# The order of matmuls inside a step of 64-wide linear attention: whole-array ones first, then scores, then values

## The chip, the cores and the metric

One core of one Trainium2 chip runs the whole program. The metric is the device time of one execution, in microseconds (us), as the median of several runs. TensorE is called PE here, its weight loads PEld, VectorE DVE, ScalarE ACT, GpSimd POOL.

## The reference

Two transformer blocks, written as one function of x (4, 512, 256): softmax attention, a mixture of experts, linear attention with 128-wide heads, the mixture of experts again, then **linear attention with 32 heads of width 64**, a choice-by-expert layer, latent attention and the choice-by-expert layer again. Each adds to x. Only the 64-wide linear attention is touched:

```
qkv = silu(h @ qkv_w.T);  q, k, v = split(qkv)          # per head
for each chunk:
    aw    = (q @ k.T) * diagonal_decay                   # scores
    intra = aw @ v                                       # values
    inter = (q * query_decay) @ state                    # the state's share
    state = state * block_decay + (k * key_decay).T @ v  # growing the state
    o     = intra + inter
out = (sigmoid(h @ gate_w.T) * rmsnorm(o)) @ out_w.T
```

## The kernel before, in words

The function `lin64_layer` works in 32 **units** w: eight groups of four heads (QUADS), for each of four batches. A unit has four **steps** n = 0 to 3, one per chunk of 128 positions. Each engine runs its own list of instructions in program order; rings of PSUM banks with a "full" and a "free" semaphore tie them together. Two rings matter: S (the scores, one pair of banks) and U ("out", a single bank). D (one bank) carries the turned k, the state's growth, the next batch turned and the mean square.

In a step (w, n), PE's part is written out by hand at the end of the tensor block:

- `product` (L1401): the projections of the next unit w + 1, q at n = 0, k at n = 1, v at n = 2, the gate and the transposes of k at n = 3. q, k and gate are two times six matmuls over 512 columns (L1433), v is 24 over 256 (L1426), in float32r; the transposes are L1408. `project` (L1484, matmuls L1492) takes the output projection of unit w - 1 at n = 1.
- `scores` (L1438, matmuls L1446) of the **next** step: four matmuls whose operands stand on 64 partitions, 64x128 weights, so that heads use the upper or the lower half of the array.
- `grow_state` (L1450, matmuls L1459), not at n = 3: two matmuls over the whole array.
- `output` (L1463): for each pair r of heads two value matmuls with 128x64 weights (L1477), each into one half of the partitions, and, except at n = 0, one whole-array matmul that adds the state's share (L1480):

```
for h in range(2):
    mm = nc.tensor.matmul(bank[halves[h], to], vs[...], am[...], start=True, stop=True)
if n:
    mm = nc.tensor.matmul(bank[:, to], state[...], qd[...], start=False, stop=True, ...)
```

A plain fp32 matmul is two records in the trace (so the two state matmuls of `grow_state` are four loads); a float32r one is one record.

What the other engines do in a step: ACT activates the products out of PSUM, then squares the out bank (L1582). DVE decays the turned k (`decay_k`, L1612), decays the next step's scores (`decay_scores`, L1619), updates the state (`keep_state`, L1633 and L1638), at n = 1 adds the output projection of unit w - 1 (`add_output`, L1660), in units 0, 1 and 31 does steps of a layer norm for a next batch, and then gates the out bank (`gate`, L1648), which sets U free. In units 29 to 31, at n = 3, PE computes a mean square (`mean_square`, L1513) and DVE an inverse root (`finish`) ahead of the scores and a scaling (`scale`, L1676) ahead of the gate. POOL decays q for the next step (`decay_q`, L1740) and adds squares (L1749). After n = 3 of units 0, 1 and 31 PE transposes a next batch (`turn_batch`, L1503), which waits for DVE's normalised x (L209).

Of the kernel before, what the change touches and what calls it, by code (L numbers as in the profile page):

```python
# [31 lines left out]
NT = T // P  # L32
# [942 lines left out]
CH = P  # L975
# [331 lines left out]
H5, D5 = 32, 64  # L1307
# [6 lines left out]
def lin64_layer(nc, c, loads):  # L1314
# [21 lines left out]
    vs = sb("vs", [P, 2, NT, 4 * D5])  # L1336
    ysum = sb("ysum", [P, B, NT, DM])
    squares = sb("squares", [P, B, 2, NT, CH])
    am = sb("am", [P, 2, 2, 2, CH])
# [3 lines left out]
    qd = sb("qd", [P, 2, 2, CH])  # L1343
    state = sb("state", [P, 2, 2, P])
# [5 lines left out]
    A, D, O, S, U = c.A, c.D, c.O, c.S, c.U  # L1350
# [23 lines left out]
    halves = (slice(0, D5), slice(D5, P))  # L1374
# [3 lines left out]
    def products_in(w, n):  # L1378

        if w + 1 == N:  # L1380
            return []
        names = [("q",), ("k",), ("v",), ("gate", "turn")][n]
        return [(name, w + 1, r) for r in range(2) for name in names]
# [4 lines left out]
    def next_batch(w, n):  # L1388

        if w < B - 2:  # L1390
            return w + 2, {0: (0, 1), 1: (2, 3), 2: (4, 5), 3: (6,)}[n]
        if w == N - 1:
            return 0, {0: (0, 1, 2), 1: (3, 4), 2: (5, 6), 3: ()}[n]
        return None

    with nc.Block() as block:
        @block.tensor
        def _(pe):
# [39 lines left out]
            def scores(w, n):  # L1438
                if n == 0:
                    pe.wait_ge(A.free.s, A.released(0, "k", w, 1))  # L1440
                pe.wait_ge(S.free.s, S.may_fill(0))
                pair = S.fill("scores", w, n)
                now = slice(n * CH, (n + 1) * CH)
                for r in range(2):
                    for h, rows_ in enumerate(halves):
                        mm = nc.tensor.matmul(pair[:, h, r * CH:(r + 1) * CH], kt[rows_, w % 2, r, now],  # L1446
                                              qs[rows_, w % 2, r, now], start=True, stop=True)
                mm.then_inc(S.full.s, 1)

            def grow_state(w, n):  # L1450
                if n == NT - 1:
                    return
                if n == 0:
                    pe.wait_ge(D.free.s, D.released(0, "turn", w, 1))
                    pe.wait_ge(A.free.s, A.released(0, "v", w, 1))
                pe.wait_ge(D.free.s, D.may_fill(0))
                bank = D.fill("state", w, n)
                for r in range(2):
                    mm = nc.tensor.matmul(bank[:, r * P:(r + 1) * P], kd_[:, r, n, :],  # L1459
                                          vs[:, w % 2, n, r * P:(r + 1) * P], start=True, stop=True)  # L1460
                mm.then_inc(D.full.s, 1)

            def output(w, n):  # L1463
                pe.wait_ge(S.free.s, S.released(0, "scores", w, n))
                pe.wait_ge(U.free.s, U.may_fill(0))
                bank = U.fill("out", w, n)
                if n:
                    pe.wait_ge(D.free.s, D.released(0, "state", w, n - 1))
                    m = w * (NT - 1) + n - 1
                    pe.wait_ge(c.qd_ready.s, c.qd_ready.at(0, m + 1))  # L1470
                else:
                    pe.wait_ge(c.set_up.s, c.set_up.at(0, 3))
                for r in range(2):
                    to = slice(r * CH, (r + 1) * CH)
                    for h in range(2):
                        head = 2 * r + h
                        mm = nc.tensor.matmul(bank[halves[h], to], vs[:, w % 2, n, head * D5:(head + 1) * D5],  # L1477
                                              am[:, n % 2, h, r, :], start=True, stop=True)
                    if n:
                        mm = nc.tensor.matmul(bank[:, to], state[:, (n - 1) % 2, r, :], qd[:, m % 2, r, :],  # L1480
                                              start=False, stop=True, skip_group_check=True)
                mm.then_inc(U.full.s, 1)

            def project(w):  # L1484
                u, b = units[w]
                for half in range(2):
                    pe.wait_ge(U.free.s, U.released(0, "out", w, 2 * half + 1))
                    pe.wait_ge(O.free.s, O.may_fill(0))
                    bank = O.fill("y", w, half)
                    for i in range(2 * half, 2 * half + 2):  # L1490
                        for r in range(2):
                            mm = nc.tensor.matmul(bank[:, (i % 2) * DM:(i % 2 + 1) * DM],  # L1492
                                                  gt[:, w % 2, r, i * P:(i + 1) * P], wo[:, 2 * u + r, :],
                                                  start=(r == 0), stop=(r == 1))
                    mm.then_inc(O.full.s, 1)

            def turn_batch(b, turn):
                pe.wait_ge(c.xn_ready.s, c.xn_ready.at(0, turn))
                for kd in range(KD):
                    pe.wait_ge(D.free.s, D.may_fill(0))  # L1500
                    bank = D.fill("xt", b, kd)
                    for i in range(NT):
                        mm = nc.tensor.transpose(bank[:, i * P:(i + 1) * P], c.xn[:, i, kd * P:(kd + 1) * P],  # L1503
                                                 c.ident[:])
                    mm.then_inc(D.full.s, 1)

            def mean_square(b):
                pe.wait_ge(c.sq_ready.s, c.sq_ready.at(0, (N - 2 * B + b + 1) * NT))
                pe.wait_ge(D.free.s, D.may_fill(0))
                bank = D.fill("mean square", b)  # L1510
                for i in range(NT):
                    for r in range(2):
                        mm = nc.tensor.matmul(bank[:, i:i + 1], squares[:, b, r, i, :], one, start=(r == 0), stop=(r == 1))  # L1513
                mm.then_inc(D.full.s, 1)
# [5 lines left out]
            for k, (w, n) in enumerate(steps):  # L1520
                for what in products_in(w, n):
                    product(*what)
                if n == 1 and w:
                    project(w - 1)
                if n == 3 and w > N - B:
                    mean_square(w - 1 - (N - B))
                if k + 1 < len(steps):
                    scores(*steps[k + 1])
                grow_state(w, n)
                output(w, n)  # L1530
                if n == NT - 1 and next_batch(w, n):
                    b = next_batch(w, n)[0]
                    turn_batch(b if w < B else "next", w + 2 if w < B else B)
# [898 lines left out]
```

## Time and profile before

| what | value |
|---|---|
| median of 3 runs | 3156.69 us (3152.51 to 3158.48) |
| the profiled execution | 3153.1 us, span 3150.4 us |
| mean granted PE clock | 0.926 of full speed |
| PE busy | 2854.7 us (91%), 15592 matmuls |
| PEld busy | 1944.5 us (62%) |
| DVE busy | 1659.8 us (53%) |
| ACT busy | 842.7 us (27%) |
| POOL busy | 992.2 us (31%) |
| products of the layer, L1433 | x1152, mean 413 ns |
| scores, L1446 | x1024, mean 301 ns |
| growing the state, L1459 | x384, mean 302 ns |
| values, L1477 | x1024, mean 300 ns |
| state's share, L1480 | x384, mean 333 ns |

Busy time counts a matmul from its start to its modelled end, and matmuls overlap in the array, so a mean duration is not the distance between two of them; the starts of the weight loads show that distance. The 64-wide layer lies between about 1600 and 2475 us of the span. A load row's "idle" is the time that the load queue stood still ahead of it; "issue" names no engine or semaphore as its cause.

### The profile page before, as it was taken

The numbers are of one execution on the slowest core, as the hardware profiler recorded it, in microseconds if no ns is written. First come the engines' busy times: TensorE is split into PE (matmuls) and PEld (weight loads), VectorE is DVE, ScalarE is ACT, GpSimd is POOL, SyncE is SP. The second block draws the span as 40 slices with busy tenths as digits, with TensorE's granted clock in tenths as the row PEclk, the third lists the DMA queues.
The fourth block names the chain that finished last, engine by engine and source line by source line (L and its number), as shares of the span: only waits on it lengthen the run. The fifth ranks groups of instructions, "written<-read, shape, count | busy, mean of one in ns | idle before, by whom it ended". The sixth has DMA issues, their size and how long they took to land. (4 is left out here: it accounts for less than half of the span.)

```text
span 3150.4 us, 45793 instructions
## 1 busy us (share of the span) xinstructions
PE 2854.7 (91%) x15592; PEld 1944.5 (62%) x15592; DVE 1659.8 (53%) x4517; ACT 842.7 (27%) x1368; POOL 992.2 (31%) x1105
## 2 busy tenths in 40 slices
PE   7999999998999999999979999999999758888876
PEld 3444458886656555788867777777777634443444
DVE  5566646666555646466644333333333565555555
ACT  2343344442101101344422222222222002222310
POOL 0000036765444445567631122222221011121211
PEclk8999999999999999999989999999999657888975
DMA  3000020000000000100000000000000000000000
GB/s 138 1 0 0 0 100 1 0 0 0 1 0 0 0 0 0 81 0 0 0 14 14 1 14 15 14 1 14 15 1 1 24 0 1 1 0 1 1 0 27
DMA packets 6288, 37.96 MB, mean 12 GB/s; under 512 B 272, under 2 KB 4368, under 8 KB 4496
## 3 DMA queue, kind: packets, MB, share of 16 engines
q1 hardware_dynamic: 6160, 36.34, 3.0%
q8 instruction: 70, 1.15, 0.1%
q14 instruction: 58, 0.48, 0.0%
HBM read 34.24 MB, written 2.10 MB: 12 GB/s over the span
## 5 line engine op out<-in xcount | busy, mean ns | idle before, releaser
L590 PE MATMUL banks<-back 32*128 32x512 f32 (+3 forms) x1088 | 364.6, 598 | 31.4 <-DVE back L600 22.1
L365 PE MATMUL banks<-moe_parts 128*128 128x512 f32 x1536 | 368.4, 396 | 15.3 <-POOL moe_parts L445 8.5
L817 ACT ACTIVATE back<-banks 128x1024 f32<-128x1024 f32 (+3 forms) x256 | 217.0, 863 | 459.7 <-PE banks L711 459.5
L365 PEld LDWEIGHTS banks<-moe_parts 128*128 128x128 f32 x1536 | 287.7, 191 | 78.5 <-issue 20.8
L1433 PE MATMUL banks<-lin_parts 128*128 128x512 f32 x1152 | 307.5, 413 | 18.9 <-DVE lin_parts L1684 15.5
L1619 DVE TENSOR_TENSOR ffn_pack<-banks,back 128x512 f32<-128x512 f32 x128 | 88.5, 691 | 351.5 <-PE banks L1446 351.4
L711 PE MATMUL banks<-back 32*128 32x512 f32 (+3 forms) x1024 | 242.3, 586 | 19.8 <-DVE back L833 12.5
L1433 PEld LDWEIGHTS banks<-lin_parts 128*128 128x128 f32 x1152 | 213.6, 194 | 67.4 <-issue 21.0
L590 PEld LDWEIGHTS banks<-back 32*128 32x128 f32 x1088 | 135.2, 199 | 187.9 <-DVE back L604 77.8
L1749 POOL TENSOR_TENSOR ffn_pack<-ffn_pack 128x256 f32<-128x256 f32 x112 | 82.9, 740 | 498.9 <-ACT ffn_pack L1582 498.9
L604 DVE TENSOR_REDUCE back<-banks 128x1 f32<-128x512 f32 x272 | 176.5, 687 | 79.9 <-PE banks L590 75.4
L379 PEld LDWEIGHTS banks<-moe_parts 128*128 128x128 f32 x1536 | 191.0, 194 | 21.7 <-issue 21.1
L379 PE MATMUL banks<-moe_parts 128*128 128x256 f32 x1536 | 202.5, 289 | 0.9
L510 DVE TENSOR_TENSOR moe<-moe,banks 128x512 f32<-128x512 f32 x128 | 87.6, 688 | 198.9 <-PE banks L365 198.9
L450 POOL TENSOR_TENSOR moe_parts<-moe,moe_parts 128x512 fp32r<-128x512 f32 x128 | 165.8, 1296 | 10.2 <-ACT moe_parts L412 10.2
L462 POOL TENSOR_TENSOR moe_parts<-ffn_pack,moe_parts 128x512 fp32r<-128x512 f32 x128 | 165.2, 1290 | 0.6 <-ACT moe_parts L432 0.4
L890 POOL TENSOR_TENSOR back<-back,small_pack 128x512 f32<-128x512 f32 x32 | 33.2, 1039 | 418.6 <-DVE back L840 418.6
L1055 PE MATMUL banks<-xt,back 128*128 128x512 f32 x320 | 148.9, 602 | 4.6 <-DVE lin L1177 2.1
L1582 ACT ACTIVATE ffn_pack<-banks 128x256 f32<-128x256 f32 x128 | 49.2, 385 | 361.8 <-PE banks L1480 322.6
L422 ACT ACTIVATE moe<-banks 128x512 f32<-128x512 f32 x128 | 76.5, 597 | 243.4 <-PE banks L365 243.3
L1154 ACT ACTIVATE lin<-banks 128x512 f32<-128x512 f32 x64 | 38.2, 597 | 369.6 <-PE banks L1104 191.2
L902 POOL TENSOR_TENSOR pool_spare<-small_pack 128x1 f32<-128x1 f32 x128 | 24.7, 193 | 349.4 <-ACT back L817 349.1
(235 smaller groups left out, 5307.0 us busy)
## 6 DMA issues: line engine op xcount, KB each, us to landing
back<-p_raw SPq DMA_DIRECT2D x8, 1024.0 KB, 4.8
back<-p SPq DMA_DIRECT2D x1, 7696.0 KB, 21.5
ffn_pack<-ffn SPq DMA_DIRECT2D x1, 6144.0 KB, 26.8
back<-p SPq DMA_DIRECT2D x1, 5152.0 KB, 15.2
back<-p SPq DMA_DIRECT2D x2, 1792.0 KB, 8.2
out<-x SPq DMA_DIRECT2D x1, 2048.0 KB, 7.5
x<-x_in SPq DMA_DIRECT2D x1, 1536.0 KB, 12.7
small_pack<-small SPq DMA_DIRECT2D x1, 619.0 KB, 4.9
```

Of the source, the lines that this page charges most:

```text
L365: mm = nc.tensor.matmul(bank[:], up[:, n % 2, a, which, kd, :], xp[:, b, kd, :], start=((a, b, kd) == (0, 0, 0)), stop=((a, b, kd) == (1, ...
L379: mm = nc.tensor.matmul(bank[:, (i % 2) * DM:(i % 2 + 1) * DM], hp[:, (e % 2) * FC + f, a, i * P:(i + 1) * P], dn[:, e % 2, b, f, :], star ...
L450: nc.gpsimd.tensor_tensor(hp[:, n % 4, 1, :], gate[:, n % 4, :], hp[:, n % 4, 0, :], ALU.subtract)\
L462: nc.gpsimd.tensor_tensor(up[:, n % 2, 1], w_up[:, (n + 2) % UNITS], up[:, n % 2, 0], ALU.subtract).then_inc(c.up_lo.s, 1)
L510: nc.vector.tensor_tensor(gate[:, (e % 2) * FC + f, :], gate[:, (e % 2) * FC + f, :], bank[:], ALU.mult).then_inc(D.free.s, 1)
L590: nc.tensor.matmul(bank[:, 0:n], qs[head_rows[j], hg, qi * P:(qi + 1) * P], ks[head_rows[j], hg, 0:n], start=True, stop=True).then_inc(D.f ...
L604: ins = nc.vector.tensor_reduce(mx[:, qi, j:j + 1], bank[:], AX, ALU.max)
L711: mm = nc.tensor.matmul(bank[:, q0:T], ks[head_rows[j], hg, kt * P:(kt + 1) * P], qs[head_rows[j], hg, q0:T], start=True, stop=True)
L817: nc.scalar.activation(pt[:, (kt % 2) * 2 + pair, :, q0:T], two[:, :, q0:T], ACT.Exp, scale=0.25).then_inc(A.free.s, 2)
L1055: mm = nc.tensor.matmul(bank[:], w[:, kd, :], c.xt[:, kd, :], start=(kd == 0), stop=(kd == KD - 1))
L1433: mm = nc.tensor.matmul(bank[:], wp[:, a, m, kd, r * P:(r + 1) * P], xp[:, b, x, kd, :], start=((a, x, kd) == (0, 0, 0)), stop=((a, x, kd) ...
L1619: nc.vector.tensor_tensor(am[:, n % 2].rearrange("p h r i -> p h (r i)"), pair[:, :, 0:2 * CH], decay[:, units[w][0]].rearrange("p h r i - ...
```

## The change

In a step, PE now issues `grow_state` of this step, then the state's share of this step's output (`from_state`), then the scores of the next step, then the values of this step (`from_chunk`). The state's share begins the sum in PSUM: its first matmul sets `start`, and the value matmuls add to it (at n = 0, where there is no state, the values set `start`). The waits go with the instructions: those for the out bank, the state and the decayed q stand ahead of the state's share, the one for the decayed scores ahead of the values.

```diff
-            def output(w, n):
-                pe.wait_ge(S.free.s, S.released(0, "scores", w, n))
+            def from_state(w, n):
                 pe.wait_ge(U.free.s, U.may_fill(0))
                 bank = U.fill("out", w, n)
-                if n:
-                    pe.wait_ge(D.free.s, D.released(0, "state", w, n - 1))
-                    m = w * (NT - 1) + n - 1
-                    pe.wait_ge(c.qd_ready.s, c.qd_ready.at(0, m + 1))
-                else:
+                if n == 0:
+                    return
+                pe.wait_ge(D.free.s, D.released(0, "state", w, n - 1))
+                m = w * (NT - 1) + n - 1
+                pe.wait_ge(c.qd_ready.s, c.qd_ready.at(0, m + 1))
+                for r in range(2):
+                    nc.tensor.matmul(bank[:, r * CH:(r + 1) * CH], state[:, (n - 1) % 2, r, :], qd[:, m % 2, r, :],
+                                     start=(r == 0), stop=True, skip_group_check=True)
+
+            def from_chunk(w, n):
+                pe.wait_ge(S.free.s, S.released(0, "scores", w, n))
+                if n == 0:
                     pe.wait_ge(c.set_up.s, c.set_up.at(0, 3))
+                bank = U.banks[U.index["out", w, n] % len(U.banks)]
                 for r in range(2):
-                    to = slice(r * CH, (r + 1) * CH)
                     for h in range(2):
                         head = 2 * r + h
-                        mm = nc.tensor.matmul(bank[halves[h], to], vs[:, w % 2, n, head * D5:(head + 1) * D5],
-                                              am[:, n % 2, h, r, :], start=True, stop=True)
-                    if n:
-                        mm = nc.tensor.matmul(bank[:, to], state[:, (n - 1) % 2, r, :], qd[:, m % 2, r, :],
-                                              start=False, stop=True, skip_group_check=True)
+                        mm = nc.tensor.matmul(bank[halves[h], r * CH:(r + 1) * CH],
+                                              vs[:, w % 2, n, head * D5:(head + 1) * D5], am[:, n % 2, h, r, :],
+                                              start=(n == 0), stop=True, skip_group_check=True)
                 mm.then_inc(U.full.s, 1)
...
+                grow_state(w, n)
+                from_state(w, n)
                 if k + 1 < len(steps):
                     scores(*steps[k + 1])
-                grow_state(w, n)
-                output(w, n)
+                from_chunk(w, n)
```

PE, a step n = 1 in the middle of the layer, with its waits, from behind the output projection to v's products; before. L1446 are scores, L1459 the state's growth, L1477 values, L1480 the state's share, L1426 products; `out_free` is the out bank's semaphore.

```order
L1446 MATMUL banks<-back 128x128 [waits score_pair_free]
L1446 MATMUL banks<-back 128x128 x3
L1459 MATMUL banks<-ffn_pack,back 128x128 [waits d_free]
L1459 MATMUL banks<-ffn_pack,back 128x128
L1477 MATMUL banks<-ffn_pack 64x128 [waits d_free,qd_ready,out_free,score_pair_free]
L1477 MATMUL banks<-ffn_pack 64x128
L1480 MATMUL banks<-lin 128x128
L1477 MATMUL banks<-ffn_pack 64x128 x2
L1480 MATMUL banks<-lin 128x128
L1426 MATMUL banks<-lin_parts 128x256 [waits a_free]
```

The same step after the change, where L1472 is the state's share and L1483 the values:

```order
L1459 MATMUL banks<-ffn_pack,back 128x128 [waits d_free]
L1459 MATMUL banks<-ffn_pack,back 128x128
L1472 MATMUL banks<-lin 128x128 [waits qd_ready,d_free,out_free]
L1472 MATMUL banks<-lin 128x128
L1446 MATMUL banks<-back 128x128 [waits score_pair_free]
L1446 MATMUL banks<-back 128x128 x3
L1483 MATMUL banks<-ffn_pack 64x128 [waits score_pair_free]
L1483 MATMUL banks<-ffn_pack 64x128 x3
L1426 MATMUL banks<-lin_parts 128x256 [waits a_free]
```

The growth and the state's share moved ahead of the scores, and with them the wait for the out bank; the values are now four in a row.

PE, step n = 3 and the first products of the next step, before (L1408 transposes, L1433 products):

```order
L1408 MATMUL banks<-small_pack,back 128x128 x4
L1446 MATMUL banks<-back 128x128 x4
L1477 MATMUL banks<-ffn_pack 64x128 x2
L1480 MATMUL banks<-lin 128x128
L1477 MATMUL banks<-ffn_pack 64x128 x2
L1480 MATMUL banks<-lin 128x128
L1433 MATMUL banks<-lin_parts 128x512 x12
```

and after:

```order
L1408 MATMUL banks<-small_pack,back 128x128 x4
L1472 MATMUL banks<-lin 128x128 x2
L1446 MATMUL banks<-back 128x128 x4
L1483 MATMUL banks<-ffn_pack 64x128 x4
L1433 MATMUL banks<-lin_parts 128x512 x12
```

Here too the state's share stands ahead of the scores, and the values follow them without a break. The lists of the other engines and of the DMA queue are unchanged but for line numbers.

## Rows read from the trace of the kernel before

**Rows 1.** 1700 to 2400 us: PE, PEld, DVE, ACT, POOL busy (count), clock, DMA share, GB/s.
```profile
1700.00:2400.00 700.00, 700.00 (x4711) 553.37 (x4709) 254.85 (x604) 186.67 (x355) 166.88 (x211) 1.00 0.03 10
```

**Rows 2.** Waits of the weight loads, 1700 to 2400 us: total us, times, longest.
```profile
PEld banks L1480 <- issue: 28.1, 164, 0.2
```

**Rows 3.** Timeline: start us, us, engine, line, operation, tiles, count; step n = 0.
```profile
1900.85 2.62 PEld L1433 LDWEIGHTS banks<-lin_parts 128*128 128x128 f32 x12
...
1903.82 0.52 PEld L1446 LDWEIGHTS banks<-back 64*128 64x128 f32 x8 [0.35 <-issue]
...
1904.46 0.52 PEld L1459 LDWEIGHTS banks<-ffn_pack,back 128*128 128x128 f32 x4
...
1905.11 0.42 PEld L1477 LDWEIGHTS banks<-ffn_pack 128*64 128x64 f32 x8
...
1905.69 2.63 PEld L1433 LDWEIGHTS banks<-lin_parts 128*128 128x128 f32 x12 [0.17 <-issue]
```

**Rows 4.** Timeline, weight loads of steps n = 1 and n = 2.
```profile
1908.37 3.44 PEld L1492 LDWEIGHTS banks<-back 128*128 128x128 f32 x16
...
1912.13 0.52 PEld L1446 LDWEIGHTS banks<-back 64*128 64x128 f32 x8 [0.33 <-issue]
...
1912.78 0.52 PEld L1459 LDWEIGHTS banks<-ffn_pack,back 128*128 128x128 f32 x4
...
1913.42 0.20 PEld L1477 LDWEIGHTS banks<-ffn_pack 128*64 128x64 f32 x4
...
1913.79 0.30 PEld L1480 LDWEIGHTS banks<-lin 128*128 128x128 f32 x2 [0.17 <-issue]
...
1914.21 0.20 PEld L1477 LDWEIGHTS banks<-ffn_pack 128*64 128x64 f32 x4
...
1914.58 0.30 PEld L1480 LDWEIGHTS banks<-lin 128*128 128x128 f32 x2 [0.17 <-issue]
...
1914.80 2.94 PEld L1426 LDWEIGHTS banks<-lin_parts 128*128 128x128 f32 x24
```

**Rows 5.** Timeline, weight loads from n = 3 to the next unit.
```profile
1920.53 1.22 PEld L1433 LDWEIGHTS banks<-lin_parts 128*128 128x128 f32 x6
...
1921.79 0.59 PEld L1408 LDWEIGHTS banks<-small_pack,back 128*128 128x128 f32 x4
...
1922.35 1.24 PEld L1433 LDWEIGHTS banks<-lin_parts 128*128 128x128 f32 x6
...
1923.62 0.59 PEld L1408 LDWEIGHTS banks<-small_pack,back 128*128 128x128 f32 x4
...
1924.37 0.52 PEld L1446 LDWEIGHTS banks<-back 64*128 64x128 f32 x8 [0.17 <-issue]
...
1925.02 0.20 PEld L1477 LDWEIGHTS banks<-ffn_pack 128*64 128x64 f32 x4
...
1926.39 2.62 PEld L1433 LDWEIGHTS banks<-lin_parts 128*128 128x128 f32 x12
```

**Rows 6.** Timeline, DVE in step n = 1: decay of scores and gate.
```profile
1912.90 0.69 DVE L1619 TENSOR_TENSOR ffn_pack<-banks,back 128x512 f32<-128x512 f32 x1 [6.25 <-PE banks L1446]
...
1915.74 0.41 DVE L1648 SCALAR_TENSOR_TENSOR back<-back,banks 128x256 f32<-128x256 f32 x1
```

**Rows 7.** Timeline, the layer's two ends.
```profile
1661.37 4.53 PEld L1433 LDWEIGHTS banks<-lin_parts 128*128 128x128 f32 x12 [1.88 <-DVE lin_parts L1596]
...
2443.93 0.93 PEld L1446 LDWEIGHTS banks<-back 64*128 64x128 f32 x8
...
2449.55 0.41 DVE L1648 SCALAR_TENSOR_TENSOR back<-back,banks 128x256 f32<-128x256 f32 x1
...
2450.09 0.67 PEld L1477 LDWEIGHTS banks<-ffn_pack 128*64 128x64 f32 x8 [0.22 <-issue]
...
2460.76 0.25 PEld L1477 LDWEIGHTS banks<-ffn_pack 128*64 128x64 f32 x4 [2.14 <-issue]
```

**Rows 8.** Stretch 1661 to 1665 us, columns as in rows 1.
```profile
1661.00:1665.00 4.00, 3.63 (x9) 2.85 (x10) 0.32 (x1) 0.60 (x1) 0.00 (x0) 0.50 0.00 0
```

## The prediction

> **What bounds the kernel now.** The page's slices say that TensorE (PE) is busy nearly all the time; the question is what happens in the stage that the change touches. I read the stretches first. From 1700 to 2400 us, inside the 64-wide layer, PE is busy in 700.00 of 700.00 us at granted clock 1.00 (2.4 GHz), DVE in 254.85, ACT in 186.67, POOL in 166.88 [rows 1]. So PE sets this stage's time, and whatever PE issues less is gained, as long as nobody becomes late. A busy row counts a matmul from start to modelled end, though, and hides how far apart matmuls start. The waits list for the weight loads gives the hint: in that stretch 164 of the loads for the state's matmuls (L1480) stand behind 0.17 us in which the load queue waits for nothing named, 28.1 us together [rows 2]. That is no semaphore; it sits where a 128x128 matmul follows a 128x64 one.
>
> Then I read one unit (one group of four heads of one batch, steps n = 0 to 3) on the weight loads, whose starts show the true pitch. Call P the step's products, G the growing of the state, S the scores (64 rows), V the values (64 columns), St the state's share; G, St and P use the whole array. The unit runs from 1900.85 to 1926.39, 25.54 us [rows 3, 5].
> - St is two loads. Before another whole-array matmul it takes 1914.80 - 1914.58 = 0.22; before V it takes 1914.21 - 1913.79 = 0.42 [rows 4]. The change of shape costs 0.20.
> - G is four such loads, so 0.43 bare, and takes 0.64 before V [rows 4]: 0.21 for the change.
> - V takes 0.37 for four loads and 0.58 for eight [rows 3, 4]. Four more loads cost 0.21, so the bare eight are 0.42 and leaving V costs 0.16. The halves run in pairs.
> - S takes 0.65, before G [rows 3, 4] and before V at n = 3 [rows 5] alike.
> - P to S also costs: twelve 512-wide loads take 2.97 to S, but 2.68 to the projection, which is whole-array [rows 3, 4]. Four transposes take 0.56 to the next product and 0.75 to S [rows 5], so 0.19.
>
> Waits that are already met cost nothing here: the transposes wait for two semaphores, and the six loads ahead of them take 1.26, 0.21 each [rows 5].
>
> The Trainium skill, TensorEngine Tiling (Array Packing), Key Properties, says that changing the tiling mode, not just the tile, drains TensorE; the trace agrees with 0.16 to 0.3 us at each change. The page TensorE: Matmul & The Clock Gate, Single matmul latency, puts what a lone warm matmul pays over its columns at 166 ns. An estimate from that page alone, over the nine changes counted below and 32 units, would be 9 x 0.166 x 32 = 48 us of gain; the rows give the sum that I use.
>
> **The change, part by part.** No instruction is added or removed; the arithmetic, ACT's, DVE's, POOL's and the DMA queue's own orders stay. PE's order within a step becomes P, G, St, S, V. Changes of shape per unit, before: n = 0 four (P-S, S-G, G-V, V-P), n = 1 and 2 six each, n = 3 five, together 21. After: three per step, 12. Step by step, from the start of P's loads to the start of the next P's:
> - n = 0: before 1905.69 - 1900.85 = 4.84 [rows 3]. After: P 2.68, G 0.43, change 0.21, S 0.65, V 0.58 = 4.55. Gain 0.29.
> - n = 1: before 1914.80 - 1905.69 = 9.11 [rows 3, 4]. After: P 2.68; the projection's 16 loads at (3.44 - 0.19) / 15 = 0.217 each, 3.47 [rows 4]; G 0.43; St 0.43 + 0.20; S 0.65; V 0.58 = 8.44. Gain 0.67.
> - n = 2: before 1920.53 - 1914.80 = 5.73 [rows 4, 5]. After: 24 loads at (2.94 - 0.19) / 23 = 0.1196, 2.87 [rows 4]; then 0.43 + 0.63 + 0.65 + 0.58 = 5.16. Gain 0.57.
> - n = 3: before 1926.39 - 1920.53 = 5.86 [rows 5]. After: up to S 3.84, less 0.19; then 0.63 + 0.65 + 0.58 = 5.51. Gain 0.35.
>
> Sum 1.88 per unit. Two prices are not in the trace. P to G is a product in fp32r followed by plain fp32 of the same shape: its ends are nothing (as P to the projection) and 0.3 (as P to S); I take nothing, since the shape is what it shares with the projection. V that adds to what St began instead of overwriting: its ends are nothing and a loss of the pairing, 4 x 0.107 = 0.43 a step; I take nothing, because each fp32 matmul here is already two records, the second adding to the first, and the pairing is there.
>
> **What gets later.** St waits for the out bank (its one buffer is released by DVE's gate of the step before), and now stands ahead of S; before, that wait stood behind S and G. Behind it are queued S, and so DVE's decay of the next scores and the next state. Tightest is n = 1 to n = 2, where DVE does decay, keep_state, the output's addition and only then the gate. Before, S starts at 1912.13, DVE's decay at 1912.90 and the gate ends at 1915.74 + 0.41 = 1916.15 [rows 4, 6], 4.02 after S; add 0.13 until PE goes on (gate end 2449.96, V 2450.09 [rows 7]): 4.15. After the change PE comes to that wait S 0.65 + V 0.58 + P 2.87 + G 0.43 = 4.53 after S. Slack 0.38, so no stall. At the other steps DVE has no additions to do (over 1.2 us less) and the slack is larger. S now starts later against the end of P (0.43 + 0.63 instead of 0.2), but decayed scores are used a whole step later. ACT squares right after V as before. POOL's decayed q is made a step ahead.
>
> The ends of the layer go otherwise, since DVE is the later one there:
> - Units 0 and 1: after n = 3 PE transposes the next batch and waits for DVE's normalised x, which comes behind the decay of S. S comes 0.63 - 0.19 = 0.44 later after P, so n = 3 loses 0.44 instead of gaining 0.35: 1.09 each, 2.2 together.
> - Unit 29: the root and the scaling ahead of the gate put its end at 2449.96 when S started at 2443.93, 6.03 later, in the same chain at unit 30's end [rows 7]. After the change, from the end of the mean square: 0.63 + 0.65 + 0.58 + 2.68 + 0.43 = 4.97 against 6.03: a stall of 1.1. Unit 29 gains 0.8.
> - Units 30 and 31: unit 31 has no products as cover. S follows each late gate instead of preceding it, and the decay, the norm steps and the gate after it move too. The values of step 2 stand idle for 2.14 until that gate now [rows 7]; S, 0.65 at full clock, comes behind it twice, at half clock more. I take 1.5 of gain for unit 30 and 2 of loss for unit 31, by estimate.
>
> Sum: 27 x 1.88 = 50.8, plus 2.2, 0.8 and 1.5, less 2.0: 53.3 us. The profiled execution took 3153.1 (span 3150.4 and 2.7 around it), so 3099.8; the median of the runs is 3.6 above it: **3103 us**, 1.7% less.
>
> **The rivals.**
> 1. *The product's format costs.* P to G keeps 0.3 at n = 0 and 0.2 at n = 2. Then 0.5 a unit is lost, 14 us over 27 units: 3117. For it: PE's long waits before S follow products. Against: P to the projection shows none [rows 3, 4].
> 2. *Adding values lose the pairing.* Three steps by 0.43 over 31 units are 40 us: 3143. For it: no V in the trace adds to another matmul's sum. Against: the second pass of each does.
> 3. *Slower: the single out bank becomes the loop.* Place: the wait ahead of St at n = 2. If the gate came 1.4 us later than I count, PE would idle 1 us per unit, and idling can bring the clock down: at 1661 us, after loads that waited 1.88, the granted clock is 0.50 (1.2 GHz) [rows 8], and twelve loads took 4.53 [rows 7] instead of 2.62 [rows 3]. At 2 us of idle and 2 us of slow product a unit pays 4.0 and gains 1.88: 27 x 2.1 = 57 us slower, 3214. It decides from 2.3 us of delay without the clock's part. Against: slack 0.38, DVE busy for 36% of the stretch [rows 1]. For: all its terms come from one unit's rows, and the wait now holds S back, which feeds the same DVE queue.
> 4. *The gain is eaten.* The drain moves instead of going away (a change from 64 rows to 64 columns being dearer than the 0.22 seen at n = 3, or PE's queue bounding elsewhere): about 3157.
>
> **How the numbers follow.** My case 0.85, rival 1 0.04, rival 2 0.04, rival 3 0.04, rival 4 0.03. A unit's gain is uncertain by 0.15 (rounding of some ten differences of 0.01, and the drain's 0.16 to 0.3), 4 us; the ends by 3; the median of runs by 3. With room for half of rival 1: 3095 to 3114. A change of 0.2%, 6.3 us, is what a measurement of this kernel can tell from none. Faster: the case, rivals 1 and 2, 0.93; same: most of rival 4, 0.03; slower 0.04.
>
> **What would show it.** The unit's period in the middle falls from 25.54 to about 23.7, PE still without idle. Loads: G 0.43 to St, St 0.63 to S, S 0.65 to V, V 0.58 to P at every n; no load of St waits 0.17. P to G leaves no gap (else rival 1); V of 0.85 or more is rival 2; idle of St's loads behind DVE's gate at n = 2 in the middle of the layer is rival 3. DVE's gate ends about 4.0 after S at n = 1. I am wrong if the period is above 24.4, or if the stages outside the layer move.

## The result and the profile after

The changed kernel took 3103.96 us (median of 4 runs, 3097.37 to 3112.98) against 3156.43 us; the ratio is 0.9837, 95% interval 0.9803 to 0.9871. Faster, clear of the noise though by less than 2%: 52.5 us in the medians; 3103 was forecast, in a range of 3095 to 3114. Its runs fall into two groups, two at 3097.4 and two at 3110.5 and 3113.0. The profiled one is the longest of them: 3112.98, span 3111.2, 39.2 under the span before. A second set of runs on one chip (experiment e5) gave 3113.49 against 3153.93, ratio 0.9873 (0.9857 to 0.9889). One of its nine runs of the kernel before was slow, at 13369 us, and is not in the ratio. Of all ten runs of the change that are on record, seven lie between 3108 and 3118 and three near 3098. So the size depends on which of them are met, 40 or 52 us, and part of the closeness of the forecast is luck. Where both come from is told below.

The middle of the layer, as in [rows 1]:

```profile
1700.00:2340.00 640.00, 640.00 (x4600) 540.23 (x4600) 247.08 (x590) 182.90 (x348) 164.28 (x207) 1.00 0.03 11
```

PE is busy in 640.00 of 640.00 us at clock 1.00, as before. The busy share tells nothing of the gain: the same work now takes less time at the same 100%. The waits of the weight loads (total us, times, longest) answer to [rows 2]. Before, from 1700 to 2400 us, the loads of the scores had one more such row:

```profile
PEld banks L1446 <- issue: 23.3, 82, 0.4
```

After, from 1650 to 2400 us:

```profile
PEld banks L1433 <- issue: 15.4, 89, 0.3
PEld banks L1426 <- issue: 5.1, 30, 0.2
...
PEld banks L1472 <- DVE back L1653: 0.8, 1, 0.8
```

The 28.1 us ahead of the loads of the state's share are gone, and of the 23.3 us ahead of the scores 0.4 are left. Nearly all that remains of that kind stands ahead of products, 15.4 and 5.1 us: the change of shape from the values. The state's share (now L1472) waits for DVE's gate once in this stretch.

The timeline of a unit in the middle, weight loads, with two PE rows and DVE's gate where they are spoken of; it answers to [rows 3 to 6]. L1459 is the growth, L1472 the state's share, L1446 the scores, L1483 the values, L1426 and L1433 products:

```profile
1900.27 0.63 PEld L1459 LDWEIGHTS banks<-ffn_pack,back 128*128 128x128 f32 x4
...
1900.82 0.53 PEld L1472 LDWEIGHTS banks<-lin 128*128 128x128 f32 x4
...
1901.47 0.52 PEld L1446 LDWEIGHTS banks<-back 64*128 64x128 f32 x8
...
1902.70 2.93 PEld L1426 LDWEIGHTS banks<-lin_parts 128*128 128x128 f32 x24 [0.17 <-issue]
...
1905.04 0.42 DVE L1653 SCALAR_TENSOR_TENSOR back<-back,banks 128x256 f32<-128x256 f32 x1
1905.56 0.53 PEld L1459 LDWEIGHTS banks<-ffn_pack,back 128*128 128x128 f32 x4
...
1906.01 0.53 PEld L1472 LDWEIGHTS banks<-lin 128*128 128x128 f32 x4
...
1907.89 1.23 PEld L1433 LDWEIGHTS banks<-lin_parts 128*128 128x128 f32 x6 [0.17 <-issue]
...
1909.16 0.58 PEld L1408 LDWEIGHTS banks<-small_pack,back 128*128 128x128 f32 x4
...
1912.84 0.42 PEld L1483 LDWEIGHTS banks<-ffn_pack 128*64 128x64 f32 x8
...
1913.42 2.63 PEld L1433 LDWEIGHTS banks<-lin_parts 128*128 128x128 f32 x12 [0.17 <-issue]
...
1916.10 0.64 PEld L1459 LDWEIGHTS banks<-ffn_pack,back 128*128 128x128 f32 x4
1916.32 0.60 PE L1459 MATMUL banks<-ffn_pack,back 128*128 128x128 f32 x4
...
1916.86 0.52 PEld L1446 LDWEIGHTS banks<-back 64*128 64x128 f32 x8
...
1917.50 0.41 PEld L1483 LDWEIGHTS banks<-ffn_pack 128*64 128x64 f32 x8
...
1918.09 2.61 PEld L1433 LDWEIGHTS banks<-lin_parts 128*128 128x128 f32 x12 [0.17 <-issue]
```

From one v product to the next it is 1926.63 - 1902.70 = 23.93 us, where it was 25.55; 27 of these intervals in a row read 23.92 or 23.93. Step by step, from the start of a product to the next product's: n = 0 takes 1918.09 - 1913.42 = 4.67, n = 2 takes 1907.89 - 1902.70 = 5.19, n = 3 takes 1913.42 - 1907.89 = 5.53, and the rest, n = 1, 8.54. Against the kernel before that is 0.17, 0.54, 0.33 and 0.57 us less, for 1, 3, 2 and 3 changes of shape fewer: 0.17 to 0.19 for each, in every step. At n = 1 the gate ends at 1905.04 + 0.42 = 1905.46 and the next state's share starts at 1906.01, so the out bank is free in time.

The whole layer, from the first v load (L1426) to the first transposes of the layer behind it (L1872 before, L1877 after), reads from these rows (minimum, median and longest ns, then first and last start); first the kernel before:

```profile
L1426 PEld LDWEIGHTS banks<-lin_parts x768: 187/192/193, 1620.9 to 2434.3; 128*128 128x128 f32 x192
L1872 PE MATMUL banks<-small_pack,xn x32: 421/421/477, 2495.5 to 3076.2; 128*128 128x128 f32 x32
```

and after:

```profile
L1426 PEld LDWEIGHTS banks<-lin_parts x768: 186/192/193, 1621.7 to 2388.4; 128*128 128x128 f32 x192
L1877 PE MATMUL banks<-small_pack,xn x32: 417/421/474, 2452.5 to 3036.9; 128*128 128x128 f32 x32
```

That is 2495.5 - 1620.9 = 874.6 us before and 2452.5 - 1621.7 = 830.8 us after: 43.8 less. The two layers behind it, whose code is untouched, run from that first row's start to its last: 580.7 us before (3076.2 - 2495.5) and 584.4 after (3036.9 - 2452.5), 3.7 more; and the layer began 0.8 later. 43.8 - 3.7 - 0.8 is the 39.2 of the spans, to 0.1.

### The profile page after: what moved, and what is told of

It is laid out like the page before. It is cut to its first block and busy times, and to the rows that moved or that the text cites. A ratio compares the mean times of both kernels' runs of the same rounds, so it can differ in the third digit from the quotient of the medians.

```text
span 3111.2 us, 45729 instructions
## 1 busy us (share of the span) xinstructions
PE 2809.1 (90%) x15592; PEld 1946.9 (63%) x15592; DVE 1653.8 (53%) x4517; ACT 843.2 (27%) x1368; POOL 991.8 (32%) x1105
## 5 line engine op out<-in xcount | busy, mean ns | idle before, releaser
L365 PE MATMUL banks<-moe_parts 128*128 128x512 f32 x1536 | 369.9, 397 | 13.8 <-POOL moe_parts L445 8.8
L1433 PE MATMUL banks<-lin_parts 128*128 128x512 f32 x1152 | 309.8, 415 | 19.3 <-DVE lin_parts L1689 15.5
L1433 PEld LDWEIGHTS banks<-lin_parts 128*128 128x128 f32 x1152 | 213.7, 194 | 77.9 <-issue 31.2
L726 PE MATMUL banks<-back 128*32 128x512 f32 (+3 forms) x1024 | 125.2, 563 | 5.3 <-POOL back L904 4.9
```

The costliest lines, as they stand in the source:

```text
L365: mm = nc.tensor.matmul(bank[:], up[:, n % 2, a, which, kd, :], xp[:, b, kd, :], start=((a, b, kd) == (0, 0, 0)), stop=((a, b, kd) == (1, ...
L726: mm = nc.tensor.matmul(bank[j * HP:(j + 1) * HP, q0:T], v[:, kt, hg * HJ + j, :], pt[:, (kt % 2) * 2 + j // 2, j % 2, q0:T], start=(kt == ...
L1433: mm = nc.tensor.matmul(bank[:], wp[:, a, m, kd, r * P:(r + 1) * P], xp[:, b, x, kd, :], start=((a, x, kd) == (0, 0, 0)), stop=((a, x, kd) ...
```

## The experiments

Two theories stood at the start. **A**: a change of the shape in which the array is used (whole, 64 rows, 64 columns) costs a fixed time, wherever it stands. With 21 changes per unit before and 12 after, 1.62 / 9 = 0.18 us each. **D** (a theory, not the bank of that name): what cost time was an addition in PSUM onto a sum just written; the old order had the state's share add to the values directly behind them. All verdicts are read from the unit's period in the middle, which is steady to 0.01 us, since the whole time scatters by more than these differences. Single executions of e1 to e4 are 7, 5, 13 and 2 us under one of the kernel before on the same chip, 3140.89, where 28, 17 and 33 were expected of the first three. That execution lies 8 us below every other one of the kernel before, at a granted clock of 0.931 against 0.922 to 0.927, and left no trace. By the traces the layer is 23.0, 15.2, 29.9 and 14.0 us shorter in them than in the trace of before.

**e1, scores first.** The change with the scores put back to the head of the step.

```diff
+                if k + 1 < len(steps):
+                    scores(*steps[k + 1])
                 grow_state(w, n)
                 from_state(w, n)
-                if k + 1 < len(steps):
-                    scores(*steps[k + 1])
                 from_chunk(w, n)
```

> The change with the scores put back at the head of the step: scores, growth, state's share, values. Shape changes per unit: 16 (before 21, the change 12). Theory A, each change of shape costs the same 0.18 us wherever it sits (1.62 us of period for 9 changes): period of a unit in the middle 25.55 - 5 x 0.18 = 24.65 us, time about 28 us under before. Rival D, the gain comes from the state's share no longer adding onto values just written in PSUM (a dependency, not a shape): all of the gain stays, period 23.93.

The loads of its step n = 1 and the next unit's v product:

```profile
1904.61 0.52 PEld L1446 LDWEIGHTS banks<-back 64*128 64x128 f32 x8 [0.33 <-issue]
1905.25 0.52 PEld L1459 LDWEIGHTS banks<-ffn_pack,back 128*128 128x128 f32 x4
1905.69 0.53 PEld L1472 LDWEIGHTS banks<-lin 128*128 128x128 f32 x4
...
1906.93 2.93 PEld L1426 LDWEIGHTS banks<-lin_parts 128*128 128x128 f32 x24 [0.17 <-issue]
...
1931.62 2.93 PEld L1426 LDWEIGHTS banks<-lin_parts 128*128 128x128 f32 x24 [0.17 <-issue]
```

Period 24.69 (24.65 by A, 23.93 by D). The four added changes cost 0.76, 0.19 each, though state's share and values keep their order. They do stand closer here, with no scores between them, so this run alone does not exclude a cost of the values' additions; e4 does. From growth to state's share it is 0.44 for four loads, the bare pitch. One execution, 3133.49 us.

**e2, growth only.** The kernel before with only the growth of the state ahead of the scores.

```diff
+                grow_state(w, n)
                 if k + 1 < len(steps):
                     scores(*steps[k + 1])
-                grow_state(w, n)
                 output(w, n)
```

> The kernel before with only the growth of the state moved ahead of the scores; values and state's share still alternate. 18 changes of shape per unit. Theory A: 25.55 - 3 x 0.18 = 25.01 us per unit, about 17 us under before. Rival D: nothing about the dependency changed, 25.55 us, no gain.

Two v products in a row:

```profile
1909.53 2.93 PEld L1426 LDWEIGHTS banks<-lin_parts 128*128 128x128 f32 x24
...
1934.49 2.93 PEld L1426 LDWEIGHTS banks<-lin_parts 128*128 128x128 f32 x24
```

Period 24.96 at this place, 24.95 over the middle (25.01 by A, 25.55 by D). Three changes fewer gave 0.60 while values and state's share still alternate. D explains nothing of this, since every addition stands where it stood. One execution, 3135.82.

**e3, values, then state.** The order of before, but the four values together and both state matmuls behind them.

```diff
                 for r in range(2):
                     for h in range(2):
...
-                                              am[:, n % 2, h, r, :], start=True, stop=True)
-                    if n:
-                        mm = nc.tensor.matmul(bank[:, to], state[:, (n - 1) % 2, r, :], qd[:, m % 2, r, :],
-                                              start=False, stop=True, skip_group_check=True)
+                                              am[:, n % 2, h, r, :], start=(r == 0), stop=True,
+                                              skip_group_check=True)
+                if n:
+                    for r in range(2):
+                        mm = nc.tensor.matmul(bank[:, r * CH:(r + 1) * CH], state[:, (n - 1) % 2, r, :],
+                                              qd[:, m % 2, r, :], start=False, stop=True, skip_group_check=True)
```

> The kernel before with its order scores, growth, but the four value matmuls together and the state's share of both pairs behind them, added to the values. 15 changes per unit. Theory A: 25.55 - 6 x 0.18 = 24.47 us per unit, about 33 us under before. Rival D, if an addition waits for the sum under it: the state's share still adds to values, only one pair further away, so between 25.55 and 24.47.

Values, state's share (L1482 here), v product, and the next unit's v product:

```profile
1905.38 0.42 PEld L1477 LDWEIGHTS banks<-ffn_pack 128*64 128x64 f32 x8
1905.97 0.52 PEld L1482 LDWEIGHTS banks<-lin 128*128 128x128 f32 x4 [0.17 <-issue]
1906.41 2.94 PEld L1426 LDWEIGHTS banks<-lin_parts 128*128 128x128 f32 x24
...
1930.93 2.94 PEld L1426 LDWEIGHTS banks<-lin_parts 128*128 128x128 f32 x24
```

Period 24.52 (24.47 by A). The state's share adds to values that were written one pair earlier, and its loads show no more than the 0.17 of the change. D had no sharp number here, so this run alone would not settle it. One execution, 3128.19.

**e4, split values.** The change, with the state's share of pair 1 put between the values of the two pairs.

```diff
+                    if n and r:
+                        nc.tensor.matmul(bank[:, CH:2 * CH], state[:, (n - 1) % 2, 1, :], qd[:, m % 2, 1, :],
+                                         start=False, stop=True, skip_group_check=True)
                     for h in range(2):
```

> The changed kernel with one half of the state's share (pair 1) taken out of the run of whole-array matmuls and put between the values of pair 0 and those of pair 1. Nothing adds to values. Two more changes in each of three steps, 18 per unit. Theory A: 23.93 + 6 x 0.18 = 25.01 us per unit. Rival D: only the values of pair 1 now add to a sum just begun, so 23.93 plus at most 3 such waits.

```profile
1910.51 0.20 PEld L1486 LDWEIGHTS banks<-ffn_pack 128*64 128x64 f32 x4
1910.88 0.30 PEld L1482 LDWEIGHTS banks<-lin 128*128 128x128 f32 x2 [0.17 <-issue]
1911.30 0.20 PEld L1486 LDWEIGHTS banks<-ffn_pack 128*64 128x64 f32 x4
1911.67 2.92 PEld L1426 LDWEIGHTS banks<-lin_parts 128*128 128x128 f32 x24 [0.17 <-issue]
...
1936.61 2.92 PEld L1426 LDWEIGHTS banks<-lin_parts 128*128 128x128 f32 x24 [0.17 <-issue]
```

Period 24.94 here and 24.95 over the middle (25.01 by A): the 0.17 of idle is back ahead of the moved loads (L1482), and the six changes cost 1.02, 0.17 each. This half of the state's share opens its own columns of the sum and adds to no values; the values of pair 1 then add to it directly behind it. The distances are those of [rows 4] all the same. From the values to the state's share it is 1910.88 - 1910.51 = 0.37, as there, where it adds to them; from the state's share to the next values 1911.30 - 1910.88 = 0.42, as there, where they add to nothing. So neither addition costs anything that the loads show. One execution, 3139.05.

Together, changes per unit and period: 21 and 25.55, 18 and 24.95 (e2, and e4 by quite another route), 16 and 24.69, 15 and 24.52, 12 and 23.93. No run lies more than 0.06 off a line of 0.18 per change. **D falls** on e2, where 0.60 went though no addition moved, and on the 0.37 and 0.42 of e4, which are the same with an addition and without. **Theory A stands**, with one limit. These versions vary only two things: leaving the 64-column values for the whole array and coming back, three times per unit between the change and e2 or e4, 1.02 / 6 = 0.17 for each change; and whole-array matmuls put between scores and values, which makes two changes out of one, 0.19 (e1) or 0.20 (e3, and e2 against before) for the one more. The change from the whole array to the scores' 64 rows stands four times in each of these versions, so what it costs was not measured; theory A takes it to be the same.

**e5, the changed kernel again**, in five rounds.

> The changed kernel again, for its own spread and for a trace of another of its executions. Theory A: period of a unit 23.93 us in every execution. What scatters the whole time (3097 to 3113) lies outside the middle of the layer: a trace near 3097 has the same period and is shorter in the stages behind the layer, by PE's granted clock. Rival: the scatter is in the layer, because the wait for the out bank is sometimes late; then the period differs between executions.

Period 23.93. The layer took 2457.2 - 1623.6 = 833.6 us here, 830.8 in the first trace; the two layers behind it 584.0. Four runs, 3110.55 to 3117.26: none was near 3097, so this set could not tell where the short executions save their time. Two more executions were traced:

**e8 and e9, the changed kernel twice more.**

> The changed kernel once more, to catch an execution near 3097 us with a trace, beside one near 3112. Expected: middle period 23.93 us in either; the difference lies where PE's clock is granted lower, in the stages behind the layer (725.5 us from the last v product to the end in the two traces so far, 718.9 in the kernel before).

> The same again. If both come out near 3112 the shorter executions stay without a trace.

e8 was a short one, 3099.21; e9 took 3108.49. e8's row of the transposes of the layers behind, and its first stretch there (busy times of PE, PEld, DVE, ACT, POOL, then clock, DMA share, GB/s):

```profile
L1877 PE MATMUL banks<-small_pack,xn x32: 421/421/477, 2452.6 to 3023.2; 128*128 128x128 f32 x32
...
2452.70:2592.70 140.00, 94.41 (x328) 62.87 (x328) 80.04 (x375) 14.84 (x22) 13.43 (x22) 0.59 0.00 1
```

The same stretch of the first trace of the change:

```profile
2452.50:2592.50 140.00, 95.67 (x305) 63.88 (x306) 78.47 (x361) 13.65 (x20) 12.38 (x18) 0.55 0.00 0
```

Period 23.93, layer 2452.6 - 1622.5 = 830.1 us, as in the long execution. The two untouched layers took 570.6 instead of 584.4: 13.8 of the 13.7 us between the two spans (3097.5 and 3111.2). In this stretch the granted clock is 0.59 against 0.55. e9 had 577.2. So by these traces the two groups of runs are the clock that PE is granted in code that the change does not touch. The rival of e5, a late wait in the layer, falls: the period is 23.93 in all four. What scatters in the layer, 830.1 to 833.6, lies at its ends, and it too goes with the granted clock: the stretch from unit 30's v product to unit 31's took 28.4 and 28.3 us at 0.94 (first trace, e8) and 29.9 at 0.89 (e5). Why the clock differs from one execution to another is open.

**e6, ends first.** In the steps where DVE is the later one the scores stand first again.

```diff
+                early = (w < B - 2 and n == NT - 1) or w == N - 1 or (w == N - 2 and n == NT - 1)
+                if early and k + 1 < len(steps):
+                    scores(*steps[k + 1])
                 grow_state(w, n)
                 from_state(w, n)
-                if k + 1 < len(steps):
+                if not early and k + 1 < len(steps):
                     scores(*steps[k + 1])
```

> The changed kernel, but in the steps where DVE is the later one (n = 3 of units 0 and 1, n = 3 of unit 30, all of unit 31) the scores stand at the head of the step as before. Theory E, the scores behind the late gate cost the ends of the layer: period unchanged at 23.93, the two head units 0.8 us each shorter, the tail about 3 us shorter, together 4 to 5 us under the change. Rival: the ends are set by the chain mean square, root, scaling, gate alone and the order there is worth nothing, 0 us.

> The version with the scores first at the layer's ends, for a second trace: if the tail is won by the order, the time from the last v product to the end is again near 718 us; if the 718.4 of the first trace was the scatter of the clock, it may as well be 725.

The start of unit 31, and the row of the layers behind:

```profile
2401.31 0.52 PEld L1446 LDWEIGHTS banks<-back 64*128 64x128 f32 x8 [0.67 <-DVE ffn_pack L1627]
...
2401.95 0.52 PEld L1459 LDWEIGHTS banks<-ffn_pack,back 128*128 128x128 f32 x4
...
2403.73 0.41 DVE L1656 SCALAR_TENSOR_TENSOR back<-back,banks 128x256 f32<-128x256 f32 x1
...
2404.19 0.56 PEld L1483 LDWEIGHTS banks<-ffn_pack 128*64 128x64 f32 x8 [1.72 <-DVE back L1656]
...
L1880 PE MATMUL banks<-small_pack,xn x32: 421/421/476, 2449.2 to 3029.9; 128*128 128x128 f32 x32
```

Scores (2401.31) and growth now stand ahead of the late gate and the values directly behind it. In the change that gate looks so:

```profile
2403.65 0.41 DVE L1653 SCALAR_TENSOR_TENSOR back<-back,banks 128x256 f32<-128x256 f32 x1
2404.11 0.52 PEld L1446 LDWEIGHTS banks<-back 64*128 64x128 f32 x8 [2.79 <-DVE back L1653]
...
2413.85 0.52 PEld L1459 LDWEIGHTS banks<-ffn_pack,back 128*128 128x128 f32 x4 [1.32 <-DVE lin L1643]
...
2416.67 0.52 PEld L1472 LDWEIGHTS banks<-lin 128*128 128x128 f32 x4 [2.30 <-DVE back L1653]
```

There the scores start at 2404.11, behind the gate, and later the growth (2413.85) and the state's share (2416.67) wait 1.32 and 2.30 on DVE. In e6 the growth no longer waits there; the state's share still does, 2.34 us. The layer takes 2449.2 - 1622.5 = 826.7 us in e6 and 826.7 again in e10, against 830.1 to 833.6 in four traces of the change: 3.4 to 6.9 less, around the 4 to 5 expected. Most of it is won in the tail: from the last v product's first load to the layer's end it is 63.4 in both, 66.7 to 67.4 in the change, 63.9 before. PE's granted clock there is 0.75 in e6 and 0.74 in the first trace of the change; by an estimate from these two numbers (0.26 of 66.8 us less 0.25 of 63.4), at most 1.5 of the 3.4 us is clock. From the first v product to the fourth it is 88.9 in both, 88.98 to 90.25 in the change. There the clock hides a gain: e6 and e10 have 88.9 at 0.88, e5 and e9 have 90.2 at 0.89, so at about the same clock 1.3 of the 1.6 expected of the head is there. The median of e6 is 3105.95 (3102.41 to 3106.65, 5 runs) against 3113.49 of e5 on the same chip; ratio to before 0.9849 (0.9835 to 0.9862). The intervals of the two just overlap, so of the whole time this is likely rather than shown; of the layer it is shown. e10's second question, whether 718.4 from the last v product to the end was scatter, came out at 715.0; but that stretch holds the untouched layers (577.3 here), so it judges nothing, and the tail of 63.4 does.

**e7, values, then scores.** The change with the two last groups exchanged.

```diff
                 grow_state(w, n)
                 from_state(w, n)
+                from_chunk(w, n)
                 if k + 1 < len(steps):
                     scores(*steps[k + 1])
-                from_chunk(w, n)
```

> The changed kernel with the values ahead of the scores: growth, state's share, values, scores. 12 changes per unit, as in the change. By theory A alone 23.93 us per unit. But the scores, and so DVE's decay, additions and gate at n = 1, come 0.58 later against PE's next wait for the out bank, where the trace of the change leaves 0.42 of slack: with the loop of the out bank closing, the state's share at n = 2 stands about 0.16 behind the gate and the period is 24.1, and the units without products lose some us more. Rival: no wait shows and the period is 23.93.

Steps n = 2 and n = 3; L1653 is the gate, L1643 the update of the state, L1408 the transposes:

```profile
1913.82 0.41 DVE L1653 SCALAR_TENSOR_TENSOR back<-back,banks 128x256 f32<-128x256 f32 x1
...
1914.28 0.52 PEld L1472 LDWEIGHTS banks<-lin 128*128 128x128 f32 x4
...
1916.16 1.23 PEld L1433 LDWEIGHTS banks<-lin_parts 128*128 128x128 f32 x6
...
1916.88 0.96 DVE L1643 SCALAR_TENSOR_TENSOR lin<-lin,back,banks 64x64 f32<-64x64 f32 x4
...
1917.96 0.42 PEld L1408 LDWEIGHTS banks<-small_pack,back 128*128 128x128 f32 x4 [0.57 <-issue]
1917.99 0.63 PE L1408 MATMUL banks<-small_pack,back 128*128 128x128 f32 x4 [0.17 <-DVE lin L1643]
```

Period 24.33 at this place, 24.33 to 24.46 over the middle: more than the 24.1 expected and clear of the rival's 23.93. The state's share does stand behind the gate, by less than 0.1 (0.53 from the growth instead of 0.45). The greater part is a wait that I had not listed: at n = 3 the transposes need bank D, which DVE frees only with the state's update, 1916.88 + 0.96 = 1917.84, and their loads stand 0.57 idle until 1917.96, the first matmul 0.17. The same wait stands in all 24 units between 1750 and 2350 us. Step by step, n = 3 takes 5.88 where the change has 5.53, n = 2 5.27 for 5.19, and the other two are within 0.03 of it. The order has no more changes of shape than the change; what it costs is waits on DVE. The layer takes 849.9 us against 830.1 to 833.6 in the change. The whole time is 3120.33 us (3117.73 and 3122.93), both above all four runs of e5, though the intervals of the ratios overlap: slower by the layer, likely by the whole.

## Why the prediction was right, and where its sizes were off

**What bounds the layer: right.** PE at 100% and clock 1.00, nobody late in the middle; only the distance between loads counted.

**The cost of a change of shape: right in kind.** The rows gave 0.16 to 0.3, the experiments 0.17 to 0.20, 0.18 on the mean. Rival 4, a drain that only moves, falls with the period. The two unknown prices came out as taken: from a product to the growth the load comes 1916.10 - 1913.42 = 2.68 behind, no gap (rival 1 falls), and the values, now adding, take 0.59 with eight loads (rival 2 falls).

**The sum per unit: mis-sized, 1.88 for 1.62.** The step that failed is "P 2.68, G 0.43, change 0.21": n = 0 was forecast at 4.55 and took 4.67, n = 1 8.44 and took 8.54 (there it is the growth behind the projection, 0.55 to the state's share instead of 0.43); n = 2 (5.16, 5.19) and n = 3 (5.51, 5.53) were nearly right. The rows after show why. Behind a long product the growth's first load starts at 1916.10 but its matmul only at 1916.32, while the product still streams; from load to scores it is 0.76, not 0.64. I measured the product to an early load and then charged the growth as if load and matmul began together, and so counted the head start as a gain: one change fewer at n = 0 was to give 0.29 and gave 0.17. The trace of before had the sign of it, since the projection's first load stands at 1908.37 [rows 4] and its first matmul at 1908.59. From matmul to matmul it is 1916.32 - 1913.42 = 2.90 to the growth and 0.54 from there to the scores; 2.90 with the 0.64 of the rows would have given 4.77, too long by 0.10, so distances between starts, of either kind, do not simply add up across a new neighbour. Over 27 units it is 50.8 forecast, 43.7 had.

**What gets later: right.** The slack at n = 1 to n = 2 was forecast at 0.38; 0.55 lies between the gate's end and the next state's share, 0.42 after the 0.13 of latency. Rival 3 falls, and e7 shows how near it is: with the scores one group later the loop just closes, for less than 0.1 us. But I had looked at the out bank alone, and bank D was nearer: in the change the first transposes start 0.40 behind the end of DVE's state update (1909.39 - 1908.99), in e7, where they wait for it, 0.15. That leaves a slack of 0.25.

**The ends: right in kind, wrong in detail.** Units 0 and 1 were to give 2.2: from the first v product to the fourth it is 89.57 before and 88.98 to 90.25 in four traces after, so 0.6 at most. The stretch with the first mean square (v product of unit 30 to that of unit 31) took 31.37 before, at a granted clock of 0.89, and 29.9 at 0.89 or 28.3 at 0.94 after: a gain of 1.5 by the order and up to 3.1 with the clock, where I had 1.88 less the stall of 1.1, 0.8. The tail from there lost 2.8 to 3.5 where I took 0.5; e6 gives that back. The sum over the layer: 53.3 forecast, 43.8 had (41.0 to 44.5 over the four traces). Of the 9.5 that are missing the middle has 7.1, units 0 and 1 have 2.2 and the tail 2.4, and the stretch before it gives 2.2 back.

**The total: closer than its terms.** The median of 3104 holds two executions near 3097; e8, the traced one of that size, had layers behind that took some 14 us less at a higher granted clock. The executions of e5 have a median of 3113.5, still in the range, by half a microsecond. One of the signs named for being wrong did come: the stages outside the layer moved, the two layers behind from 580.7 to 584.4 us in the first trace and to 570.6 in e8. Their code is the same; the forecast had 3 us for the median of the runs, and the runs spread over 15.6.

The estimate beside it, 48 us for nine changes over 32 units, took as the price of a change the 166 ns that the Trainium skill (TensorE: Matmul & The Clock Gate, Single matmul latency) gives for what a lone warm matmul pays over its columns. The 43.8 of the layer is nearer to it than to the 53.3 of the rows, in part because the ends gave nothing; per change it is 0.166 against 0.18 measured in the middle.

## What to carry to other kernels

Count the changes of array shape (whole, part of the rows, part of the columns) in PE's order; here, at a granted clock of 1.00, each costs about 0.18 us that no busy row shows, so matmuls of one shape belong together even when that costs them their natural pairing. Before regrouping, list every bank whose release stands behind the moved work, not only the one whose wait moves. And price the regrouping by the number of changes that go, checked against whole steps, and not by adding distances between starts from different neighbourhoods: behind a product a load stood 0.22 us ahead of its matmul. Where another engine sets the pace, as at the layer's ends, keep the order that feeds it first.

## What the runs showed of the hardware that I had not expected

Changes of shape cost about the same in the two places that were varied: 0.19 each for the four that e1 adds around the scores, 0.17 for the six that e4 adds between values and state's share. An addition in PSUM directly behind the write that it adds to costs nothing that the loads show: 0.37 us from values to state's share with it (rows 4) and without (e4), 0.42 from state's share to values without (rows 4) and with it (e4). The same untouched code, some 580 us of it behind the layer, took 570.6 to 584.4 us from one execution to another, with PE's granted clock (0.55 and 0.59 in its first 140 us); that scatter of 14 us is a third of the layer's gain, so a change of this size is judged in its own stage.
